# Choosing the next free PSUM bank by an estimate of read times, and turning normalised rows earlier, in a four-layer transformer on one core

## The reference

```python
ada = silu(c) @ W_ada + b_ada                 # 6 shifts, scales and gates of 288
h = layernorm(x) * (1 + scale) + shift
q, k, v = split(h @ W_qkv + b_qkv)            # 16 heads of 18
x = x + gate * (softmax(q k^T / sqrt(18)) v @ W_proj + b_proj)
h = layernorm(x) * (1 + scale2) + shift2
x = x + gate2 * (gelu(h @ W1 + b1) @ W2 + b2) # hidden 1152
```

## Time and profile before

| what | us |
|---|---|
| median of 3 runs | 2263.82 (2252.39 to 2264.69) |
| the profiled execution, span from its first to its last instruction | 2257.0 |
| TensorE matmul busy in it | 2033.0 (90%) |
| VectorE busy | 1335.6 (59%) |
| ScalarE busy | 1143.6 (51%) |
| TensorE, mean granted clock | 0.932 of full |

### The profile page before, as it was taken

The page is one execution under the profiler, slowest core; times in us unless marked ns, Lnnn a source line. Parts: engine busy times, 40 slices in busy tenths (PEclk is TensorE's granted clock), DMA queues, the critical chain, the costliest instruction groups (busy, mean ns, idle before and its releaser), DMA issues.

```text
span 2257.0 us, 38969 instructions
## 1 busy us (share of the span) xinstructions
PE 2033.0 (90%) x15592; PEld 1509.0 (67%) x15592; DVE 1335.6 (59%) x2940; ACT 1143.6 (51%) x1705; POOL 207.4 (9%) x311
## 2 busy tenths in 40 slices
PE   6978899899989998999799899899888898999898
PEld 4347388658966994788375657788786556464658
DVE  4757637756774767476556673462444849484833
ACT  2444624574655456445626464552443464637373
POOL 2000001202100211012010000011000000000001
PEclk9787989899989999999889999998898998999999
DMA  5333332343333233333322313346254141314011
GB/s 158 77 123 57 100 95 72 79 111 86 89 77 106 72 89 76 96 94 88 94 72 35 103 17 65 73 88 109 34 95 130 7 121 26 99 11 115 9 14 25
DMA packets 204731, 173.97 MB, mean 77 GB/s; under 512 B 54822, under 2 KB 164678, under 8 KB 204550
## 3 DMA queue, kind: packets, MB, share of 16 engines
q1 hardware_dynamic: 197974, 158.76, 30.1%
q0 software_dynamic: 6576, 12.71, 2.1%
HBM read 125.57 MB, written 40.11 MB: 73 GB/s over the span
## 4 chain that ended last, share of the span: by engine, by line
PE 63%; DVE 18%; ACT 12%; DMA 3%; issue 2%; SPq 2%; POOL 0%; ACTq 0%; POOLq 0%; DVEq 0%
PE PSA L1856 16%; PE PSA L1871 13%; DVE MX L1496 7%; PE PSA L1647 5%; PE PSA L1760 5%; PE PSA L1737 5%; ACT PB L1345 4%; PE PSA L1707 4%; PE PSA L1750 4%; PE PSA L1719 2%; DVE FL L1396 2%; PE PSA L1780 1%; ACT FH L1375 1%; PE PSA L1670 1%; DVE HH L1626 1%
## 5 line engine op out<-in xcount | busy, mean ns | idle before, releaser
L1496 DVE TENSOR_REDUCE MX<-PSA 128x1 f32<-128x512 f32 x768 | 490.4, 682 | 296.9 <-PE PSA L1737 293.2
L1856 PE MATMUL PSA<-A,FH 128*128 128x256 f32 x2520 | 445.3, 292 | 12.5 <-DVE HH L1626 9.6
L1871 PE MATMUL PSA<-FH,HH 128*128 128x288 f32 x2016 | 447.7, 313 | 2.0 <-DVE HH L1626 2.0
L1382 ACT ACTIVATE HH<-PSA 128x512 fp32r<-128x512 f32 x252 | 150.4, 597 | 572.5 <-PE PSA L1856 567.3
L1345 ACT ACTIVATE PB<-PSA 128x1024 f32<-128x1024 f32 x384 | 370.9, 1025 | 102.5 <-PE PSA L1750 101.8
L1856 PEld LDWEIGHTS PSA<-A,FH 128*128 128x128 f32 x2520 | 364.9, 195 | 34.6 <-issue 17.3
L1871 PEld LDWEIGHTS PSA<-FH,HH 128*128 128x128 f32 x2016 | 329.7, 195 | 42.3 <-issue 38.0
L1871 PE MATMUL PSA<-FL,HH 128*128 128x288 f32 x1008 | 303.7, 301 | 0.0
L1737 PE MATMUL PSA<-KS,QS 54*128 54x512 f32 x768 | 226.1, 517 | 40.0 <-DVE MX L1496 14.0
L1255 POOL TENSOR_TENSOR X<-X,TM 128x288 f32<-128x288 f32 x128 | 101.1, 808 | 1496.7 <-DVE TM L1561 1496.6
L1760 PE MATMUL PSA<-PB,VT 128*32 128x512 f32 x1536 | 219.6, 637 | 0.0
(11 more groups left out here) (166 smaller groups left out, 2261.5 us busy)
## 6 DMA issues: line engine op xcount, KB each, us to landing
qkd<-HH SPq DMA_DIRECT2D x48, 504.0 KB
ST<-in_L_cond_w SPq DMA_DIRECT2D x51, 432.0 KB
ST<-in_L_cond_w SPq DMA_DIRECT2D x102, 192.0 KB
QS<-qkd SPq DMA_DIRECT2D x88, 144.0 KB
KS<-qkd SPq DMA_DIRECT2D x88, 144.0 KB
QS<-qkd SPq DMA_DIRECT2D x144, 72.0 KB
KS<-qkd SPq DMA_DIRECT2D x144, 72.0 KB
ST<-in_L_cond_w SPq DMA_DIRECT2D x153, 48.0 KB
```

The source lines that it names most:

```text
L1382: e.activation(r(HH[u][:, 0, :]), PS[bk][:, :], gelu)
L1496: e.reduce_max(MX[p // 2 % 2][:, col:col + 1], PS[bk][:, :], axis=AX.X).then_inc(free[bk], 1)
L1856: m = e.matmul(PS[bk][:, s_ * 256:(s_ + 1) * 256], r(w_), r(x_[:, half * 256:(half + 1) * 256]), start=(z == 0), stop=(z == 6))
L1871: m = e.matmul(PS[bk][:, 0:C], r(HH[u][:, c, tk]), r(w_), start=False, stop=(j == NCH - 1 and z == 2))
```

## The change

`plan` keeps a second, finer account of time, the class `Clock`: `put` passes each step to `clock.step`, which adds a fixed duration to the time of TensorE, ScalarE or VectorE and keeps for each bank when it would be full and when it would be read. A bank that TensorE has filled and nobody has yet read in the list has the read time NEVER. `ring()` now takes that bank of the present ring which is free first. Banks that would be free when TensorE arrives tie, and among these the old turn decides. Banks handed out and not yet filled come last. The banks of fc1, fc2, the values and the score pairs stay fixed. And `mid(i)` now ends with `turn_x` of unit i + 2 for every i (i + 2 < 16), after the last fc1 of unit i - 1; `pre` then skips it.

```diff
+class Clock:
+    HOP, NEVER = 110, 1e12
+    def on_pe(self, ns, mode, bk, *needs):
+        at = max([self.pe] + [n + self.HOP for n in needs] + ([self.read[bk[0]] + self.HOP] if bk else []))
+        if mode != self.mode:
+            at, ns, self.mode = at + 100, ns + 105, mode
+        self.pe = at + ns
+        if bk:
+            self.given.discard(bk[0])
+            self.last[bk[0]], self.full[bk[0]], self.read[bk[0]] = bk[1], self.pe + 150, self.NEVER
...
+    def step(self, kind, a):
...
+        elif kind == "s1":
+            _, p, _, x, bk, _ = a
+            self.on_pe(108, 64, bk, self.qk[min(p // 2, 2)])
+        elif kind == "s1_max":
+            bk = a[3]
+            self.read[bk[0]] = self.on_dve(605, self.full[bk[0]] + 100)
...
+        elif kind == "qk":
+            _, _, bk, u, _, _, ready, _, _ = a
+            self.on_pe(1630, 128, bk, self.ready_at(ready))
+            self.on_act(587, self.full[bk[0]], self.hh[u])
+        elif kind == "qk_lo":
+            bk, u = a[2], a[3]
+            self.read[bk[0]] = self.on_dve(686, self.act)
...
 def plan(full, s_av, s_tn, s_fc2, s_qw):
+    clock = Clock()
     def put(*a):
         steps.append(a)
         pe[0] += PE_NS.get(a[0], 0)
+        clock.step(a[0], a[1:])
...
     def ring():
         ring_n[0] += 1
-        return bank(ring_of[0][ring_n[0] % len(ring_of[0])])
+        x = ring_n[0] % len(ring_of[0])
+        order = ring_of[0][x:] + ring_of[0][:x]
+        return bank(min(order, key=lambda k: (k in clock.given, max(clock.read[k], clock.pe))))
...
-        if (i + 1) // 4 == 2:
+        if i + 2 < NI:
             while last_fc1[0] < i - 1:
                 yield
             yield from turn_x(norm_of[i + 2], i % 2, (i + 2) // 4, 0, (i + 2) % 4)
```

More of the change, by code:

```diff
@@ L76, in wait_ge, with __init__, on_act, on_dve @@
             self.e.wait_ge(sem, count)
+class Clock:
+    HOP, NEVER = 110, 1e12
+    QK_OUT, QK_IN, ROWS_IN = 3500, 7000, 2600
+    def __init__(self):
+        self.pe = self.act = self.dve = 0
+        self.mode = None
+        self.last = [-1] * 8
+        self.read = [0] * 8
+        self.given = set()
+        self.full = [0] * 8
+        self.xn = self.o = self.qk_out = self.v_in = 0
+        self.stat = [0, 0]
+        self.hf, self.hh, self.lo = [0] * 2, [0] * 3, [0] * 3
+        self.qk, self.rows, self.pb = [0] * 3, [0] * 4, [0] * 3
+        self.turned = {}
+        self.os = 0
+    def on_pe(self, ns, mode, bk, *needs):
[6 more added lines that the diff above has]
+            self.last[bk[0]], self.full[bk[0]], self.read[bk[0]] = bk[1], self.pe + 150, self.NEVER
+    def on_act(self, ns, *needs):
+        self.act = max((self.act,) + needs) + ns
+        return self.act
+    def on_dve(self, ns, *needs):
+        self.dve = max((self.dve,) + needs) + ns
+        return self.dve
+    def free_at(self, bk):
+        return self.read[bk[0]] if bk is not None and self.last[bk[0]] == bk[1] else 0
+    def ready_at(self, ready):
+        if ready is None:
+            return 0
+        if ready[0] == "tn":
+            return self.turned.get(ready[1], self.NEVER)
+        return self.free_at(ready[1])
+    def step(self, kind, a):
+        if kind == "fc1":
+            _, _, bk, ready, _, u, _ = a
+            self.on_pe(1650, 128, bk, self.ready_at(ready))
+            self.on_act(597, self.full[bk[0]], self.hh[u])
+            self.on_act(593)
+        elif kind == "hid":
+            bk, _, u = a
+            self.read[bk[0]] = self.lo[u] = self.on_dve(682, self.act)
+        elif kind == "fc2":
+            _, j, _, t, bk, (hb, _), u, s_ = a
+            self.on_pe(400 if j else 530, 128, None, self.lo[u], 0 if j else self.read[bk[0]])
+            if j == NCH - 1:
+                self.full[bk[0]] = self.pe + 150
+            if t and s_:
+                self.hh[u] = self.pe
+        elif kind == "res":
+            bk = a[2]
+            self.read[bk[0]] = self.on_dve(480, self.full[bk[0]])
+        elif kind == "resmid":
+            bk = a[2]
+            self.read[bk[0]] = self.on_dve(450, self.full[bk[0]])
+            self.on_dve(460, self.dve + 30)
+        elif kind == "s1":
[4 more added lines that the diff above has]
+            self.read[bk[0]] = self.on_dve(605, self.full[bk[0]] + 100)
+        elif kind == "rows":
+            _, g, bk, last, _ = a
+            self.on_pe(60, 128, bk, self.free_at(last))
+            self.read[bk[0]] = self.on_dve(550, self.full[bk[0]])
+            self.rows[g] = self.dve + self.ROWS_IN
+        elif kind == "s2":
+            _, st, p, bk, _, _ = a
+            b = bk[0]
+            self.on_pe(215, 64, bk, self.rows[st // 4], self.read[b + 1])
+            self.read[b] = self.read[b + 1] = self.on_act(915, self.full[b] + 60, self.pb[st % 3])
+        elif kind == "av":
+            _, st, hh, (eb, _), _, bk = a
+            if hh == 0 and st % 4 == 0:
+                self.on_pe(0, 32, bk)
+            self.on_pe(213, 32, None, self.read[eb])
+            if hh == 3:
+                self.pb[st % 3] = self.full[bk[0]] = self.pe + 180
+        elif kind == "os":
+            bk = a[2]
+            self.read[bk[0]] = self.os = self.on_act(594, self.full[bk[0]])
+        elif kind == "no":
+            _, _, ob, bk = a
+            self.on_pe(440, 128, bk, self.os)
+            self.read[bk[0]] = self.o = self.on_dve(745, self.full[bk[0]])
+        elif kind in ("turnx", "turnx2"):
+            c, bk = a[0], a[3]
+            self.on_pe(440, 128, bk, self.xn)
+            if kind == "turnx":
+                f = a[6]
+                self.read[bk[0]] = self.on_act(784, self.full[bk[0]], self.hf[f])
+            else:
+                self.on_act((1520, 1520, 2260)[c], self.full[bk[0]])
+        elif kind == "turnx_lo":
+            c, _, bk, f, _ = a
+            self.hf[f] = self.on_dve((1140, 1140, 1510)[c], self.free_at(bk))
+            self.turned[len(self.turned) + 1] = self.dve
+        elif kind == "turnx2_lo":
+            bk = a[2]
+            self.read[bk[0]] = self.on_dve(685, self.act)
+        elif kind == "turno":
+            c, bk = a[0], a[3]
+            self.on_pe(440, 128, bk, self.o)
+            self.on_act((594, 594, 1150)[c], self.full[bk[0]])
+        elif kind == "turno_lo":
+            bk = a[2]
+            self.read[bk[0]] = self.on_dve(685, self.act)
+        elif kind == "qk":
[5 more added lines that the diff above has]
+            self.read[bk[0]] = self.on_dve(686, self.act)
+            self.hh[u] = self.qk_out = self.dve + self.QK_OUT
+        elif kind == "qkin":
+            i, p0, p1, grp, _, need = a
+            self.qk[grp] = max(self.qk_out, self.full[need[0]] if need else 0) + self.QK_IN
+        elif kind in ("v", "v2", "proj"):
+            bk = a[2]
+            self.on_pe(930, 128, bk, self.ready_at(a[3]))
+            if kind != "proj":
+                self.read[bk[0]] = self.on_act(401, self.full[bk[0]])
+        elif kind == "bn":
+            self.on_dve(660)
+        elif kind == "rs":
+            self.on_dve((1040, 500, 500)[a[0]])
+        elif kind == "nb":
+            self.stat[a[0]] = self.on_dve(270)
+        elif kind == "xn":
+            self.xn = self.on_act(2470, self.stat[a[1]])
+        elif kind == "split":
+            self.on_act(750)
+        elif kind == "fix":
+            self.on_dve(1040)
+        elif kind == "ada":
+            bk = a[5]
+            self.on_pe(900, 128, bk)
+            self.read[bk[0]] = self.on_dve(450, self.full[bk[0]])
+        elif kind == "rt":
+            bk = a[1]
+            self.on_pe(3300, 128, bk, self.ready_at(a[2]))
+            self.read[bk[0]] = self.on_dve(174, self.full[bk[0]])
+        elif kind == "rtk":
+            self.on_dve(600)
+        elif kind == "qk2":
+            bk, f = a[2], a[3]
+            self.on_pe(1630, 128, bk, self.ready_at(a[5]))
+            self.read[bk[0]] = self.on_act(587, self.full[bk[0]], self.hf[f])
+            self.hf[f] = self.act + self.QK_OUT
+        elif kind == "s1b":
+            for bk in a[3]:
+                self.on_pe(900, 27, bk)
+        elif kind == "s1b_max":
+            bk = a[3]
+            self.read[bk[0]] = self.on_dve(686, self.full[bk[0]])
+        elif kind == "s2b":
+            for bk in a[3]:
+                self.on_pe(900, 27, bk, *self.rows[0:2])
+        elif kind == "rows2":
+            self.rows[a[1]] = self.on_dve(186) + self.ROWS_IN
+        elif kind == "s2b_exp":
+            bk = a[2]
+            self.read[bk[0]] = self.on_act(604, self.full[bk[0]])
+        elif kind == "av2":
+            for bk in a[2]:
+                self.on_pe(1300, 33, bk, *[self.free_at(b) for b in a[3].values()])
+        elif kind == "no2":
+            bk = a[4]
+            self.on_pe(440, 128, bk, self.os)
+            self.read[bk[0]] = self.on_dve(720, self.full[bk[0]])
+        elif kind == "otr":
+            self.o = self.dve + 7500
@@ L113, in bank @@
         fills[k] += 1
+        clock.given.add(k)
```

## The result

The changed kernel takes 2286.92 us (median of 5 runs, 2274.12 to 2293.81) against 2258.38 (2252.39 to 2264.69) before: a ratio of 1.011, with a 95% interval of 1.0076 to 1.0145. By that ratio it is 25 us slower (the two medians lie 28.5 us apart), where a time 35 us lower was forecast. The profiled execution is its fastest, 2274.12 us, so the two traces lie only 15.3 us apart; its mean granted clock is 0.927, and that of the other four executions is 0.916 to 0.919.

What follows compares the result with a forecast made beforehand. TensorE was taken as the bound, with VectorE breaking into its chain and the clock as second loss. The terms summed to -34.4 us on a 2257.0 us span, 2222.6, plus 6.8 outside it: 2229 us, range 2186 to 2272.

Steps and rivals of the forecast that it cites:

- The step that failed: Attention: q/k three steps earlier, 0 to 32 us gained by s1, against 5 for SP's in-order queue; both taken as 0.
- part 2: Ten turns moved from attention to the feed-forward's end: -6, -5, +12.6 and +4 us, q/k's earlier start 0.
- The bank terms: TensorE's waits for ring banks: all 15.2 us before q/k gained, and 16.8 us, half of 33.6, before s1.
- cost of a wrong choice: Bank choice for s1: 25 us if a tenth of the pairs err by one reduction; taken as 0.
- The turns: Feed-forward ends: first q/k wait -6, transposes in idle time -5, VectorE backlog +12.6, late `mid(11)` +4 us.
- The clock: Half-clock stretches behind idle TensorE: shorter stalls and more overlap spare two, at about 4 us each, 8 us gained.
- A: VectorE's backlog takes over at the feed-forwards' ends and the clock falls there: slower, 2281 us; chance 16%.
- the marks named: Signs of a wrong forecast, among them TensorE idle above 3 us behind layer 1 and 3 feed-forwards, clock 0.50 behind it.
- B: Banks are freed, VectorE isn't; s1's 33.6 us return as other VectorE waits: no change, 2253 us; chance 17%.
- D: The bank estimate doesn't steer, ties keep the old turn, only the moved turns act: 2269 us; chance 5%.
- C: All stalls go and the clock follows: far faster, 2189 us; chance 16%.

Runs made afterwards that it cites:

- kernel 5: The changed kernel with the gate row's load (GB<-GR) issued in the tenth attention step, not the fourth, in layers 0, 1 and 3: 0.9954 of the kernel before, 2245.13 us.
- 10: The kernel before the change, with only the gate row's load moved from the fourth to the eighth attention step, between its q/k stores: ratio 1.0094, 2281.28 us.
- experiment 11: Early turns with banks in the fixed turn, and the gate row's load in the tenth attention step: 1.0037 of the kernel before, 2266.73 us.
- 1: The kernel before plus the bank choice by estimate alone, turns where they were: ratio 0.9967, 2249.91 us.
- 7: The bank choice alone, with layer 2's attention back on the fixed turn of banks: 0.9919 of the kernel before, 2237.61 us.
- kernel 9: The whole change with two mends, the gate row's load in the tenth attention step and layer 2's attention on the fixed turn: 0.9898 of the kernel before, 2238.07 us.
- experiment 12: The changed kernel with the gate row's load in the first attention step, not the fourth, in layers 0, 1 and 3: 0.9984 of the kernel before, 2252.77 us.

## Why the prediction was wrong

**The step that failed** is the last of part 2: "q/k starts three steps earlier, and so do its stores, its `qk_in` loads and the s1 of the next unit", for which "I take 0 for both". It weighed SyncE's order only as a tenth of that engine's share in the chain, 5 us. It listed every DMA that moves and not the one that stays: the gate load in the fourth attention step. The runs showed that this early start put the second q/k store of eight attentions beside that load, and held SyncE's queue for the read-back until 7.0 to 9.1 us behind the store in place of 2.9. Experiments 5 and 10 price the meeting from both sides, 1.011 to 0.9954 (35 us) when it is taken out of the changed kernel, and 0.94% (21 us) when it is put in the kernel before. Out of the turns alone it takes 0.76% (17 us, experiment 11). What else the loop issues in the fourth to sixth step, and the DMA share behind 664.30 in the trace before, would have shown it ahead of the run.

**The bank terms** (-15.2 and -16.8). As waits they came: q/k behind HH and OT 15.2 to none (2.1 us behind a reduction came instead), s1's 33.6 to 16.9, half as taken. As time they didn't. The choice alone gave 0.33%, 7.4 us, not 32. With layer 2 exempted it gave 0.81%, 18 us. The "cost of a wrong choice", taken as 0 with 25 kept for the range, was therefore real: 12 us in the attentions of layer 2, by the profiles of 1 and 7. Another part went to the scores at the feed-forwards' ends, whose fixed banks 4 and 5 the estimate hands to s1 (their wait for its reductions is 6.9 us before and 15.8 with the choice alone). That leaves some 4 us of the 32 without a named place.

**The turns** (-6, -5, +12.6 and +4, together +5.6 us). This part was near in sum: without the meeting, turns alone cost 0.37% (0.19 to 0.55), 8 us. Item by item it was less good, so the nearness is in part luck. Of the first q/k wait 7.8 us became 5.4, not 1.8. TensorE's 2.1 us of transposes, which were to fit in the idle time behind three feed-forwards of layer 0 (-5), didn't fit in the kernel after: the ends before units 2, 3 and 4 grew by 2.4, 2.4 and 3.6 us. The backlog of VectorE was not underrated: of the 32 us that came to the ten ends, 21 are the transposes moved there and 4.4 the end before unit 12, where `mid(11)` is late (4 forecast), which leaves 7 for a backlog taken at 12.6.

**The clock** (-8). It went the other way: 25 us more at the half level in the profiled execution, and more in the rest, for at the median clock of 0.919 it is 2 x (1 - 0.919) x 2285 = 370 us against 307. New stalls of 3 to 5 us stand right ahead of low stretches: 0.83 in the 10 us from 690, and 0.66 in the 10 us behind the idle 4.1 us before unit 6, where the kernel before has 0.83. That the stalls cause the whole difference isn't shown. Nor did the mends give the clock more than the kernel before has: the profile of kernel 9 has 0.940, but it is the fastest of six, and their median, 0.931, is that of the kernel before on the same chip.

**The rivals.** A had the sign, and its price of 2281 is near the measured 2287, but that is luck, for its mechanism isn't what cost the time. Its sign was there to see (TensorE idle 4 us behind the feed-forwards of layers 1 and 3, one of the marks named), and kernel 5 has the same idle ends and is faster than before. B is half true of the choice: banks were freed, and much of the time came back as other waits for VectorE. D is out, since the table of waits changed. C stays unreached, with 2238 for the best version.

What stays open: how far the early turns help once the meeting is gone. Kernels 7 (without them) and 9 (with them) have overlapping intervals and didn't run on the same chip together, so no gain by them is shown. And no run puts the load late in the kernel before, where it meets no first q/k store, so what the late place may give by itself, in 5, 9 and 11, is bounded only by experiment 12: the early place gives 28 of the 35 us, and its shortfall stands mostly in unit 2.

## What to carry to other kernels

When a step is moved, list not only the DMAs that move with it but those that stay where it arrives, and look at the DMA share and GB/s behind each of them: a high share at a low rate is a load that will delay its neighbours. Moving such a load only helps if it meets nothing else: put ahead of the attention it held up a weight load. Where stores are read back, a delay of 4 us on a store holds an in-order queue and comes out as a wait of another engine, under another name in each kernel. Waits of TensorE that vanish from the table are no time saved until a run of that part alone says so; here the choice alone removed 28 us of them (9.5 before q/k, 18.7 before s1) and was worth 7.

## What the runs showed of the hardware

One row of 288 floats in SBUF copied to 128 partitions by one DMA (144 KB) keeps the DMA engines busy for more than half of some 8 us at 20 to 23 GB/s. It lands after 7.0 us there, and after 8.8 us beside the stores in the kernel after. Its neighbours land late: the second q/k store of unit 3 takes 7.35 us, and a 36 KB weight load beside two such copies 10.3 us. Plain stores of q/k in the windows of kernel 5 move 131 GB/s at a share of 0.39, and plain weight loads from DRAM, issued by GpSimd, land in 2.7 us (108 KB) and 3.2 us (288 KB) by the median of the largest groups, the slowest kind in 5.3 us. So the size alone doesn't make the copy slow. The Trainium skill (DMA: Bandwidth & Descriptors, "Measured (HBM→SBUF, 128 partitions, SWDGE, issued from GpSimd)") gives 0.95 us of DMA time for a plain 64 KB transfer to 128 partitions, from DRAM and issued by GpSimd; no trace here times a plain load of 64 KB. Whether it is the repeated source row, the one source partition or the queue that makes the difference isn't shown.
